# Adaptive-LayerNorm transformer block on one core: K's bias row by VectorE instead of TensorE, and earlier statistics of x

## The reference

```
mod = silu(c) @ wmod                      # sa, ca, ga, sb, cb, gb: rows per sequence
h   = layernorm(x) * (1 + ca) + sa
Q = elu(h@Wq+bq)+1 ; K = elu(h@Wk+bk)+1 ; V = h@Wv+bv          # 16 heads of 8
KV = sum_tokens K^T V ; Z = 1/(Q . sum K + 1e-6) ; att = (Q KV Z) @ Wo + bo
y = layernorm(h + att)*g1+beta1 ; y = layernorm(y + relu(y@W1+b1)@W2+b2)*g2+beta2
x2 = x + ga*y
h2 = layernorm(x2)*(1+cb)+sb ; mixes of h2 with its previous token (mu_r, mu_k)
out = x2 + gb * sigmoid(mix_r@W_r^T) * (relu(mix_k@W_k^T)^2 @ W_v^T)
```

## Time and profile before

| | |
|---|---|
| median of 3 runs | 163.07 us (162.75 to 163.19) |
| the profiled execution | 162.81 us, its span 160.7 us |
| PE / PEld busy | 97% / 90% of the span |
| DVE / ACT / POOL busy | 77% / 79% / 65% |
| granted TensorE clock | full in every slice |
| chain that ended last | 93% of it on PE |

### The profile page before, as it was taken

One profiled execution on the slowest core, in us unless ns is written; L12 is line 12 of the kernel. 1 busy time (PEld: TensorE's weight loads), 2 busy tenths in 40 slices (PEclk: granted clock), 3 DMA queues, 4 the chain that ended last, 5 costly groups with the idle time before them and its releaser, 6 DMA issues.

```text
span 160.7 us, 4111 instructions
## 1 busy us (share of the span) xinstructions
PE 155.6 (97%) x1151; PEld 145.1 (90%) x1151; DVE 123.1 (77%) x572; ACT 127.3 (79%) x346; POOL 104.6 (65%) x243
## 2 busy tenths in 40 slices
PE   7899999999999999999999999999999999999992
PEld 6778998999999999999999999999999999888891
DVE  3766878597887969696978779796969777888842
ACT  4256777889797979898997979797989989656562
POOL 4337567576676767787676767676877755973631
PEclk9999999999999999999999999999999999999999
DMA  4926299920010101010100101010101001010112
GB/s 122 269 90 174 67 276 369 423 115 0 2 37 0 33 0 33 4 37 0 34 5 0 33 4 35 0 35 4 33 0 35 4 0 33 2 37 0 35 33 67
DMA packets 8974, 9.94 MB, mean 62 GB/s; under 512 B 724, under 2 KB 7416, under 8 KB 8952
## 3 DMA queue, kind: packets, MB, share of 16 engines
q1 hardware_dynamic: 8656, 9.60, 18.8%
q10 hardware_dynamic: 296, 0.08, 0.2%
HBM read 7.55 MB, written 2.13 MB: 60 GB/s over the span
## 4 chain that ended last, share of the span: by engine, by line
PE 93%; DMA 2%; DVE 2%; ACT 1%; issue 0%; SPq 0%; DVEq 0%
PE bank L1266 16%; PE bank L1156 16%; PE bank L1145 8%; PE bank L1238 5%; PE bank L1194 5%; PE bank L1150 5%; PE bank L1222 4%; PE bank L1182 4%; PE bank L1230 4%; PE bank L1378 4%; PE bank L1210 4%; PE bank L1206 4%; PE bank L1249 3%; DMA kqvo<-in_kqvo 2%; PE bank L1219 1%; PE bank L1398 1%
## 5 line engine op out<-in xcount | busy, mean ns | idle before, releaser
L1156 PE MATMUL bank<-w,hid 128*128 128x128 f32 x240 | 31.7, 275 | 0.0
L1266 PE MATMUL bank<-x1T,w 128*128 128x256 f32 x120 | 30.9, 381 | 0.0
L1156 PEld LDWEIGHTS bank<-w,hid 128*128 128x128 f32 x240 | 29.3, 192 | 0.0
L347 ACT ACTIVATE hid<-bank,b_cols 128x256 f32<-128x256 f32 x60 | 26.0, 511 | 1.1 <-PE bank L1266 1.1
L544 POOL TENSOR_TENSOR rstd_n<-vare_n,power 128x2 f32<-128x2 f32 x30 | 23.8, 792 | 2.4
L1266 PEld LDWEIGHTS bank<-x1T,w 128*128 128x128 f32 x120 | 21.5, 190 | 2.7 <-DVE z L803 0.2
L710 DVE TENSOR_SCALAR ny<-bank,mv_ny,rstd_ny 128x128 f32<-128x128 f32 x32 | 11.7, 406 | 9.0 <-POOL rstd_ny L544 9.0
L323 ACT ACTIVATE hT<-bank,modT 128x256 f32<-128x256 f32 x16 | 9.0, 565 | 11.3 <-PE bank L1145 11.3
L540 POOL TENSOR_TENSOR vare_n<-mv_n,eps 128x2 f32<-128x2 f32 x30 | 5.9, 195 | 17.2 <-DVE mv_n L704 17.1
L292 ACT ACTIVATE n<-x_all,shift_n,rstd_n 128x128 f32<-128x128 f32 x27 | 11.8, 485 | 2.5 <-POOL shift_n L552 2.5
L317 ACT ACTIVATE keepT<-bank,modT 128x255 f32<-128x255 f32 x26 | 13.1, 555 | 0.0
(11 more groups left out here) (187 smaller groups left out, 454.7 us busy)
## 6 DMA issues: line engine op xcount, KB each, us to landing
gm_rows<-mod_rows_dram SPq DMA_DIRECT2D x2, 960.0 KB, 9.5
out<-out_sb SPq DMA_DIRECT2D x15, 128.0 KB, 1.8
gm_rows<-mod_rows_dram SPq DMA_DIRECT2D x1, 768.0 KB, 6.7
w<-in_w SPq DMA_DIRECT2D x1, 512.0 KB, 5.6
x_all<-in_x SPq DMA_DIRECT2D x1, 512.0 KB, 5.6
bv_row<-bv_rows_dram SPq DMA_DIRECT2D x1, 512.0 KB, 7.1
bv_row<-bv_rows_dram SPq DMA_DIRECT2D x1, 384.0 KB, 4.4
gm_rows<-mod_rows_dram SPq DMA_DIRECT2D x1, 384.0 KB, 3.7
```

The source lines that it names most:

```text
L347: last = nc.scalar.activation(hid[:, f, :], bank[:, f % 2 * L:(f % 2 + 1) * L], ACT.Relu, bias=b1_cols[:, f:f + 1])
L1156: last = nc.tensor.matmul(banks[6][:, c * D:(c + 1) * D], hid[:, f, c * 128:(c + 1) * 128], w2[:, f, :], start=False, stop=(f == FF - 1 an ...
L1266: return nc.tensor.matmul(bank[:, f % 2 * L:(f % 2 + 1) * L], w1[:, f * 128:(f + 1) * 128], x1T[:, :], start=True, stop=True)
```

## The change

1. The bias matmul in bfloat16 is gone from `k_product`. For sequence 0 a float32 matmul of a row of ones with `bias_rows` takes its place (256 columns). For sequences 1 to 15 VectorE adds `bias_rows` (128x128, repeated over both chunks) to bank 4 and writes a new SBUF tile `kb` (`k_biased`). ScalarE's exp and VectorE's elu of K read `kb` instead of bank 4. The preparation of the two bfloat16 parts and its tiles are gone; the bias is loaded to 128 partitions instead of 3.
2. In `step(t)` VectorE's order is new: `centred`, denominators, reciprocals, `k_biased`, attention, the mix for k ahead of k_elu, the mix for r after the statistics of x2. The statistics of x leave the start of the step: those of sequence t+2 are made near its end.
3. GpSimd's `first_scale` moves with them to behind the scales of n3 and ny; the deviation and shift of n1 have two buffers.
4. In the opening, n1 of sequence 0 is made once by VectorE in (x-mean)*rstd form for the transposes, and once by ScalarE for the state product; two warm-up matmuls are gone; direct_row and q_product change places; ScalarE's raw columns, exp of Q and relu of Q move by a place or two.

```diff
@@ k_product (TensorE)
+                if s == 0:
+                    pe.wait_ge(const_dve, 6)
+                    pe.wait_ge(bias_rows_ok, 1)
+                    nc.tensor.matmul(chunked(banks[4]), ones_row[:, :], bias_rows[:, :].unsqueeze(1).broadcast_to([128, NC, D]),
+                                     start=True, stop=False)
+                elif s == 1:
+                    pe.wait_ge(k_ok, 1)
                 need(pe, hT_ok, s + 1)
-                need(pe, k_ok, s)
+                need(pe, kb_ok, s - 1)
                 need(pe, tanh_ok, s - 4)
-                nc.tensor.matmul(chunked(banks[4]), ones3[:, :], bias_parts[:, :].unsqueeze(1).broadcast_to([128, NC, D]),
-                                 start=True, stop=False)
...
@@ k_exponent (ScalarE)
-                need(act, k_mm, s + 1)
-                nc.scalar.activation(exp_k[:, :, :], chunked(banks[4]), ACT.Exp, bias=neg1[:, :]).then_inc(expk_ok, 1)
+                if s == 0:
+                    act.wait_ge(k_mm, 1)
+                need(act, kb_ok, s)
+                source = kb[:, :, :] if s else chunked(banks[4])
+                nc.scalar.activation(exp_k[:, :, :], source, ACT.Exp, bias=neg1[:, :]).then_inc(expk_ok, 1)
...
@@ VectorE
+                plain = kb[:, :, :] if s else chunked(banks[4])
+                nc.vector.scalar_tensor_tensor(k_sb[:, :, :], exp_k[:, :, :], 1.0, plain, ALU.min, ALU.max).then_inc(k_ok, 1)
+
+            def k_biased(s):
+                need(dve, k_mm, s + 1)
+                need(dve, bias_rows_ok, 1)
+                nc.vector.tensor_tensor(kb[:, :, :], chunked(banks[4]), bias_rows[:, :].unsqueeze(1).broadcast_to([128, NC, D]),
+                                        ALU.add).then_inc(kb_ok, 1)
...
@@ first_steps (VectorE)
                 attention(1)
+                k_biased(2)
                 y_norm(0)
...
@@ step (VectorE)
+                if live(t):
+                    centred(sp_)
+                    denominators(sb_)
+                    reciprocals(sb_)
+                    k_biased(sa)
+                    attention(sb_)
...
@@ step (GpSimd)
-                if live(t + 1):
-                    first_scale(sa + 1)
+                if t == 3:
+                    first_scale(4)
...
+                if live(t + 2):
+                    first_scale(sa + 2)
```

More of the change, by code:

```diff
@@ L76, in build @@
         bv_rows = sb("bv_rows", [S, D])
[L77 to L82, removed]
+        bk_rows, bias_rows = sb("bk_rows", [128, D]), sb("bias_rows", [128, D])
         x_all = sb("x_all", [128, S * NC, D])
@@ L96, in build @@
         wv_plus = [sb(f"wv_plus{p}", [128, D + H]) for p in range(2)]
-        mean_r, shift_n1, one_pair = (sb(n, [128, NC]) for n in ("mean_r", "shift_n1", "one_pair"))
+        mean_r, one_pair = (sb(n, [128, NC]) for n in ("mean_r", "one_pair"))
+        rstd_n1, shift_n1 = ([sb(f"{n}{p}", [128, NC]) for p in range(2)] for n in ("rstd_n1_", "shift_n1_"))
         kvs = sb("kvs", [128, D + H])
@@ L285, in _, with n1_part, take_n1 @@
             act.dma_start(bv_pad[0:1, :], a["bv"].rearrange("(a d) -> a d", a=1)).then_inc(bv_loaded, 16)
-            def take_n1(s, chunks=range(NC)):
+            def n1_part(s, c):
+                return nc.scalar.activation(n1[s % 2][:, c, :], x_all[:, NC * s + c, :], ACT.Identity,
+                                            scale=rstd_n1[s % 2][:, c:c + 1], bias=shift_n1[s % 2][:, c:c + 1])
+            def take_n1(s):
                 need(act, aks_mm, s - 1)
@@ L290, in take_n1 @@
                 wait_x(act, s)
-                for c in chunks:
-                    last = nc.scalar.activation(n1[s % 2][:, c, :], x_all[:, NC * s + c, :], ACT.Identity,
-                                                scale=rstd["n1"][:, c:c + 1], bias=shift_n1[:, c:c + 1])
+                for c in range(NC):
+                    last = n1_part(s, c)
                 last.then_inc(n1_ok, 1)
-            take_n1(0, (0,))
+            act.wait_ge(x_in[0], 16)
+            act.wait_ge(shift_n1_ok, 1)
+            n1_part(0, 0)
             act.wait_ge(cols_ok, 2)
@@ L360, in first_steps @@
             def first_steps():
-                h_turned(0)
+                act.wait_ge(hT_mm, 1)
+                nc.scalar.activation(hT[0][:, :], banks[0][:, 0:L], ACT.Identity, scale=mod_col(CA, 0),
+                                     bias=shift_first[:, :]).then_inc(hT_ok, 1)
+                n1_part(0, 1).then_inc(n1_ok, 1)
                 k_exponent(0)
@@ L708, in normalise @@
                 need(dve, rstd_ok[name], count)
+                scale = rstd_n1[0] if name == "n1" else rstd[name]
                 for c in range(NC):
-                    last = nc.vector.tensor_scalar(dest[:, c, :], source(c), mv[name][:, c, 0:1], rstd[name][:, c:c + 1],
+                    last = nc.vector.tensor_scalar(dest[:, c, :], source(c), mv[name][:, c, 0:1], scale[:, c:c + 1],
                                                    ALU.subtract, ALU.mult)
@@ L907, in first_steps @@
                 reciprocals(0)
+                k_biased(1)
                 attention(0)
+                direct_weights(1)
                 k_elu(1)
@@ L942, in step @@
                 step_end(t - 1)
-                y_first = t == S
-                if live(t + 1):
-                    x_stats(t + 1)
-                    need(dve, stats_ok["n1"], sa + 2)
+                if live(t):
[4 more added lines that the diff above has]
+                    attention(sb_)
+                    if live(t - 4):
+                        mix_half(K_W, sc)
+                    k_elu(sa)
+                    middle(sp_)
+                    need(dve, x2_ok, sp_ + 1)
+                    norm_stats("n3", lambda c: x2_p[:, c, :])
+                    if live(t - 4):
+                        mix_half(R_W, sc)
+                    norm_mv("n3", sp_ + 1)
+                    y_stats(sb_)
+                    q_elu(sa)
+                    norm_mv("ny", sb_ + 1)
+                    if live(t + 2):
+                        x_stats(t + 2)
+                        x_mv(t + 2)
+                    masked_state(sa)
+                    shift_of_n3(sp_)
+                    y_norm(sb_)
+                    return
@@ L963, in step @@
-                if live(t):
-                    k_elu(sa)
                 middle(sp_)
-                if y_first:
-                    y_stats(sb_)
-                    norm_mv("ny", sb_ + 1)
+                y_stats(sb_)
+                norm_mv("ny", sb_ + 1)
                 need(dve, x2_ok, sp_ + 1)
                 norm_stats("n3", lambda c: x2_p[:, c, :])
-                if live(t - 4) and not draining(t):
-                    mix_half(K_W, sc)
-                    mix_half(R_W, sc)
                 norm_mv("n3", sp_ + 1)
-                if not y_first:
-                    y_stats(sb_)
@@ L977, in step @@
[L977 to L990 removed]
+                y_norm(sb_)
+                gated(sc)
```

136 lines of the change are left out of this document (52 added, 84 removed).

## The result

The changed kernel takes 165.22 us (median of 4 runs, 164.95 to 165.34) against 163.13 us of the kernel before beside it: ratio 1.0139, 95% interval 1.0120 to 1.0159. The profiled execution took 165.18 us, with a span of 163.5 us; before it was 162.81 and 160.7.

The account below looks back on a forecast made before the run. It took two equal paths to bound the steady step: TensorE's work and the chain through ScalarE's attT. Steady steps +1.2, opening +0.1 and step 3 +0.2 made +1.5 on 162.81, so 164.3 us (163.6 to 165.0; 8 in 10: 162.5 to 165.4).

Parts of the forecast that it names:

- The two paths of the steady step: Steady step: TensorE's own work, and the chain from ny's transposes through ScalarE's attT to the output product, equally long.
- Bias matmuls worth nothing in the steady steps: Steps 4 to 15: TensorE reaches the output product 0.11 us sooner but waits there for attT; worth 0 us.
- kb late by 0.06, source 0.04, 0.10 a step: Steady steps: exp K waits 0.06 us for VectorE's kb, its SBUF source costs 0.04; +1.2 us over twelve steps.
- The opening, +0.1: Opening: transposes start 0.3 us sooner, but the lead is spent by step 2's hidden products; +0.1 us, bounds -0.4 and +0.3.
- Steps 2 and 3, the rest of +0.1 and +0.2: Step 2: exp K behind k_biased, within the opening's +0.1; step 3: exp K 0.65 us later, costing +0.2.
- The sum for exp K: Steps 2 and 3: VectorE and semaphore times added up put exp K at 18.13 and 27.0 us.
- the lead it was to spend: Opening: 0.3 to 0.4 us gained by earlier n1 transposes, held up to sequence 1's attention, spent in step 2.
- The rest of the steady step at nothing: Steady step: VectorE's extra instruction, GpSimd's scales, stores and mixes cost 0, hidden by TensorE's and ScalarE's chain.
- A: Rival: TensorE is paid back at the output product's load, 0.11 us a step; faster, 161.2 us; chance 0.13.
- B: Rival: kb in time in steady steps, stall 0, SBUF source 0.04 us a step; 163.4 us; chance 0.23.
- C: Rival: as B, and the opening's lead survives, steady steps at 0 to 0.04 us; about 162.7 us; chance 0.08.
- D: Rival: steady step locked to VectorE, kb later, 0.17 to 0.2 us a step; 165.5 us; chance 0.08.

Follow-up runs that it names:

- e3: Kernel before with the bias matmul left out from sequence 3 on, nothing in its place; 162.74 us, ratio 0.9980.
- e4: Changed kernel with ScalarE's attT ahead of the first hidden copy from step 3 on; 163.79 us, ratio 1.0029.
- e8: Kernel before, bias matmul kept, with attT ahead of the first hidden copy from step 3 on; 163.26 us, ratio 1.0029.
- e12: Kernel of e11 with n1's transposes ahead of the last feed-forward matmul and prod ahead of z's statistics, from step 3 on; 161.87 us, ratio 0.9961.
- e7: Changed kernel with exp K reading PSUM in every sequence, still behind the wait for the biased copy; 163.55 us, ratio 1.0069.
- e2: Kernel before with K's bias loaded to 128 partitions (64 KB) instead of 3, nothing else changed; 164.78 us, ratio 1.0032.
- e5: Changed kernel with K's bias loaded as one row and spread by TensorE, replacing the last warm-up matmul; 163.92 us, ratio 1.0086.
- e6: Changed kernel with sequence 2's biased K made ahead of attention(1) on VectorE instead of behind it; 165.22 us, ratio 1.0140.
- e9: Kernel before, opening kept, with the biased copy right behind rden replacing the bias matmul from sequence 3 on, bias row loaded late; 164.89 us, ratio 1.0136.
- e10: Kernel of e9 with attT ahead of the first hidden copy from step 3 on; 164.84 us, ratio 1.0131.
- e1: Changed kernel with eight warm-up matmuls at the start instead of six; 164.44 us, ratio 1.0075.
- e11: Changed kernel with the edits of e4, e5 and e6 together; 162.41 us, ratio 0.9990.

## Why the prediction was right in sign and wrong in its terms

The median rose by 2.1 us to 165.22, where the forecast was +1.5 and 164.3. It lies above the forecast's own range (163.6 to 165.0) and only 0.2 us inside the wide one (162.5 to 165.4). The two paths of the steady step were read rightly; that the total came so near is partly luck, as the terms show.

- *Bias matmuls worth nothing in the steady steps*: right, shown by e3. The reason given, attT, is half of it. e4 and e8 together show it: an earlier attT gives 0.13 us a step without the bias matmul and 0.01 with it. I had not seen the second reason. In the changed kernel K's first product follows hT at once, and its second record comes after 0.164 us instead of 0.112: 0.05 us of the 0.11 are lost there, which the bias matmul had covered. e12, which also moves prod, covers it with another matmul and gets it back (8.71 to 8.67).
- *kb late by 0.06, source 0.04, 0.10 a step*: attT starts 4.11 us after the n1 transposes instead of 4.015, so +0.095, as forecast. Its parts were +0.03 for kb's lateness (the copy takes 0.36 us and exp K starts 0.03 behind its end, I took 0.41 and 0.04) and +0.06 from exp K to exp Q, of which e7 shows 0.04 to be the source, as forecast. But attT itself took 0.39 us instead of 0.42, so the load moved only by some 0.065: 0.7 us over steps 4 to 15 where I had 1.2.
- *The opening, +0.1*: the step that failed. It was 1.43 us at attT of step 1. Taken apart by traces: the 64 KB load 0.41 (e2), the long slow stretch 1.19 (e7 against the changed kernel, one trace each), the new order -0.17 (what remains; e5 shows the sign). In the new opening the load costs 0.59 (e7 14.44 less e5 13.85). I had costed the bias load at nothing, as I did not count its packets against those of Wk and Wq, which start beside it. And I cleared the warm-up matmuls with "stood in a wait", without asking for TensorE's pace. The transposes of n1 started at 7.17, not at 6.15.
- *Steps 2 and 3, the rest of +0.1 and +0.2*: 0.61 us from step 1 to step 3. The sum for exp K was of the right kind, the lead it was to spend did not exist, and ny stands behind the copy (e6): some 0.4 of the 0.61 us are there, the rest I did not take apart.
- *The rest of the steady step at nothing*: nothing in the trace speaks against it for the changed order, and e9 shows what that order hides.
- The rivals: A is refuted by e3. B (kb in time) was nearly right for the steady steps: kb held exp K back by 0.03 us only, and B's 0.5 us is nearer to the measured 0.74 than my 1.2; its total, 163.4, fails on the opening. So does C, whose lead was not there. D's total, 165.5, is nearer to the result than mine, but for the wrong reason: kb starts 2.23 us after the transposes (2.2 forecast), and the steps lose 0.06 us and not 0.2.

In sum +0.74 in steps 4 to 15 and +2.09 ahead of them, in place of +1.2 and +0.3: two errors of opposite sign, the second much the larger. On the time it came to +2.4 us in the profiled execution, since 0.4 us less lie outside its span.

**Open**: what sets the end of the slow stretch. e9 and e10 have the same instructions on TensorE up to there, and it ended at about 7.2 us in one and at 4.4 in the other; in e1 it lasted to 7.3 with next to no idle time. The Trainium skill ("TensorE: Matmul & The Clock Gate", the part on the HAM clock gate) says that the number of slow matmuls at a kernel's start varies from run to run; the traces agree. The kernel before, in its 92 executions beside the experiments, never showed a span above 161.8, while e2's load alone brought eight of twelve to 162.4 or more. The changed opening with the small load (e5, e11, e12) had twelve long executions in 31. So the load and the changed opening both make a long one likelier by these counts; how, I cannot say.

## What to carry to other kernels

Work taken off the busiest engine is worth what the next wait leaves of it: look whether a weight load of its stands right behind another engine's write (0.05 us here), and move that write first. A matmul may cover the latency of another engine's write, as the bias matmul did for hT; when it goes, put something in its place. Count the packets of a load in the opening, however small its tensor, and compare an opening by several executions, since one trace shows only one of several courses it can take.

## What the runs showed of the hardware

- TensorE's pitch for one f32 record of 128 columns was 0.213 us from the first matmul to between 4.4 and 9.4 us, and 0.112 from there on, at a granted clock of 1.00 throughout; the end differed by over 3 us between executions with the same matmuls.
- A load of one 512-byte row to 128 partitions on ScalarE's queue put the first product, which needs the 128 KB loads of Wk and Wq beside it, back by 0.5 us (4.80 in e2 against 4.28), and by 1.0 us against the 3.82 of other traces with the small load.
- ScalarE gave way after 0.42 us with a source in SBUF and 0.37 with one in PSUM (128 x 256 exp with a bias column). VectorE's sum of a PSUM and an SBUF source of this shape took 0.36 us, where the scalar_tensor_tensor that I took it from has 0.42 in the earlier trace rows.
